# Limiting the record scatters of a mixture-of-experts kernel to two in flight

## The chip, the cores and the metric

The kernel runs on one core of one Trainium2 chip. The metric is the device time of one execution in microseconds (us). The kernel before took 806.48 us (median of 3 runs, 805.17 to 807.34). Five engines matter: PE (TensorE, matrix products), DVE (VectorE), ACT (ScalarE), POOL (GpSimd) and SP (SyncE, which here only issues DMA transfers). They run their own instruction streams and meet at semaphores.

## The reference, cut to what matters

The input has 4 x 1024 = 4096 rows of 256 values. A cross-attention block comes first, then a feed-forward block with 8 experts, of which each row uses two, and one shared expert that every row uses:

```
x = x + xattn(layernorm(x), ctx, ...)
xf = layernorm(x).reshape(-1, D)
scores = softmax(xf @ gate_w.T)
_, idx = top_k(scores + gate_b, 2)
rw[t, idx] = scores[t, idx]
h = silu((xf @ w1 + b1) * (xf @ w3 + b3))
oe = h @ w2 + b2
y = sum over e of rw[t, e] * oe[t, e]
z = expert(xf, sw1, sb1, sw3, sb3, sw2, sb2)
x = x + y + z
```

## The kernel before, in words

The rows are cut into NT = 32 tiles of 128. The attention stage works tile by tile and writes, for each tile, the result row block and its normalised copy (`xn2`) to DRAM. The router then works on all 32 tiles at once on DVE: softmax of the gate products, the two best experts of a row, and for each row and each of its TOP = 2 choices a **slot** in a table of 71 units of 128 places. A unit is a tile of 128 gathered rows that all go to one expert. There are NU = 2 * 32 + 7 = 71 units.

The **record scatter** (lines 621 to 629, POOL) writes the table. `record[:, t, k, :]` has, for each of 128 rows, eight bytes: the row's number and its weight. One indirect DMA puts the 128 records of one tile and one choice at their slots in the DRAM table `slots_scratch`; there are 32 * 2 = 64 such scatters, issued one behind the other. All of them add to one semaphore, `scat_out`. POOL then waits for all 64 and loads the table back with one DMA (line 629, semaphore `slots_in`).

The **feed-forward stage** is a software pipeline of steps over 103 tiles: 20 shared tiles first (R0 = 20), then the 71 routed units, then the last 12 shared tiles. In step s, PE does for tile s - 4 the second product (line 1092, three terms and three chunks, weights ws2 or w2), for tile s the transpose of its input (line 1239), for tile s - 3 the transpose of the hidden values (line 1247), and for tile s - 1 the first product (line 1092 again, 12 matmuls, weights ws13 or w13). ACT and DVE take each result from PSUM: ACT line 812 and DVE line 951 make the high and low part of the transposed input, DVE lines 969 and 972 add the bias and multiply, ACT line 822 is silu, ACT line 817 and DVE line 956 split the hidden values, and DVE line 945 adds a shared tile's result to its row block. PE signals each of its results with a semaphore (`Y_ok`, `X_ok`, `H_ok`, `UV_ok`).

Beside the first steps, SP loads the weights of the eight experts (lines 481 to 487, issued from 325.8 us on) and their biases (line 490), and ACT (lines 785, 787) and DVE (lines 992, 995) split those weights.

For routed units POOL gathers the rows (line 634), six units ahead: gather u waits on `X_ok` for tile 20 + u - 7, and the first gather also needs the loaded table, since it comes behind line 629 and its wait on POOL. Later POOL adds results to DRAM (line 641) between gathers. So the order on POOL is: 64 scatters, the table load, six gathers, then pairs of scatter-add and gather.

Of the kernel before, what the change touches and what calls it, by code (L numbers as in the profile page):

```python
# [20 lines left out]
def wait(eng, sem, n):  # L21

    if not isinstance(n, int) or n > 0:
        eng.wait_ge(sem, n)


def xattn_moe(nc, x, ctx, Wq, Wk, Wv, Wo, bo, gate_w, gate_b, w1, b1, w3, b3, w2, b2,
              sw1, sb1, sw3, sb3, sw2, sb2, out):
    B, N, D = x.shape
    _, NK, DC = ctx.shape  # L30
    INNER = Wq.shape[1]
    DH = 64
    HEADS = INNER // DH
    E, _, H = w1.shape
    TOP = 2
    T = B * N
    NT = T // P
# [33 lines left out]
    with stack:  # L71
        def sb(name, shape, dt, on=stack):
            return on.enter_context(nc.sbuf_tensor(name, shape, dt))

        def sem(name):
            return stack.enter_context(nc.semaphore(name))
# [7 lines left out]
        record = sb("record", [P, NT, TOP, 2], I32)  # L84
# [211 lines left out]
        rank_ok = sem("rank_ok")  # L296
        slot_ok = sem("slot_ok")
        eid_ok = sem("eid_ok")
        scat_out = sem("scat_out")
        slots_in = sem("slots_in")  # L300

        raw_in = [sem(f"raw_in{e}") for e in range(E)]
# [90 lines left out]
        def w_pieces(kind, j, name):  # L393

            if kind == "O":
                return [{"raw": wo_raw, "high": woh, "low": wol}[name][:, j, :]]
            w = {"K": {"raw": wk_raw, "high": wkh, "low": wkl}, "V": {"raw": wv_raw, "high": wvh, "low": wvl}}[kind][name]
            return [w[0:n, i, j * P:(j + 1) * P] for i, (_, n) in enumerate(KC)]
# [123 lines left out]
        def _(pool):  # L522
# [99 lines left out]
            pool.wait_ge(slot_ok, 1)  # L622
            for t in range(NT):
                for k in range(TOP):
                    pool.indirect_dma_start(slots_dram, bass.IndirectOffsetOnAxis(ap=slot[:, k, t:t + 1], axis=0),  # L625
                                            record[:, t, k, :], None).then_inc(scat_out, 16)

            pool.wait_ge(scat_out, 16 * TOP * NT)
            pool.dma_start(slots[:, :, :], slots_dram.rearrange("(p n) c -> p n c", p=P)).then_inc(slots_in, 16)

            def gather(u):
# [671 lines left out]
```

## Time and profile before

| what | value |
|---|---|
| median of 3 runs | 806.48 us |
| the profiled execution's own time | 811.39 us |
| its span, first to last instruction | 809.5 us |
| mean granted TensorE clock | 0.934 |
| PE busy | 675.1 us, 83% |
| DVE busy | 535.4 us, 66% |
| ACT busy | 396.9 us, 49% |
| POOL busy | 423.1 us, 52% |

The profile is of one execution. Its own time is what the device reports for that run, and 1.9 us of it lie outside the span. Times in the rows count from the start of the span. A row of the timeline has the start in us, the duration in us, the engine, the line, the operation, the destination and source, and in brackets the idle time of the engine before it with what ended the wait. "Issue" is time in which the engine waited for nothing that the profile shows; "remote" is a semaphore that arrived from a source or at a time that the profile can't tie to an instruction's end. DMA rows name the queue: q1 carries the transfers issued by SP, q0 those issued by POOL.

### The profile page before, as it was taken

How to read it: one execution, taken by the hardware profiler on the slowest of the kernel's cores; microseconds unless marked ns; L12 is line 12 of the kernel's file. 1: busy time of each engine (PE TensorE's matmuls, PEld its weight loads, DVE VectorE, ACT ScalarE, POOL GpSimd, SP SyncE). 2: the span in 40 equal slices, each digit the busy share in tenths (PEclk: the TensorE clock that was granted, in tenths of full speed). 3: DMA queues.
4: the chain of work that ended last, by engine and by line, in shares of the span. 5: the costliest groups of instructions: out<-in, count | busy, mean ns of one | idle time of the engine just before them, and what ended most of it. 6: DMA issues, size and time to landing. Idle time of an engine off the chain costs nothing.

```text
span 809.5 us, 16280 instructions
## 1 busy us (share of the span) xinstructions
PE 675.1 (83%) x4635; PEld 633.8 (78%) x4636; DVE 535.4 (66%) x1053; ACT 396.9 (49%) x1287; POOL 423.1 (52%) x532
## 2 busy tenths in 40 slices
PE   3996899999999996603007888999999999999995
PEld 2785799999999985602007878999999999999994
DVE  3884888888888874810008888666666666666678
ACT  3995777787778772301007322343444434434432
POOL 4353866556556643377750120667667777676300
PEclk9997999999999999765558999999999999999998
DMA  9202333222222212990002321344444444445595
GB/s 214 80 1 104 129 126 88 77 66 79 66 75 71 66 56 85 296 335 11 1 4 82 106 80 53 60 79 72 72 71 72 77 69 73 73 83 109 88 370 227
DMA packets 65005, 79.96 MB, mean 99 GB/s; under 512 B 11337, under 2 KB 57906, under 8 KB 64946
## 3 DMA queue, kind: packets, MB, share of 16 engines
q1 hardware_dynamic: 47618, 55.81, 22.7%
q0 software_dynamic: 15744, 18.84, 14.7%
q10 hardware_dynamic: 1584, 4.59, 1.5%
q8 instruction: 30, 0.49, 0.2%
q14 instruction: 29, 0.24, 0.1%
HBM read 49.97 MB, written 29.24 MB: 98 GB/s over the span
## 4 chain that ended last, share of the span: by engine, by line
PE 74%; another core or an unknown queue 9%; DVE 8%; issue 3%; DMA 3%; ACT 2%; POOL 1%; SPq 0%; ACTq 0%; DVEq 0%; POOLq 0%
PE ps L1092 62%; PE ps L1247 4%; PE ps L1175 3%; PE ps L1239 2%; PE ps L1152 1%; DMA wq_sb<-in_L_xattn_Wq 1%; DMA xrow<-xn_scratch,slots 1%; DVE w13l L992 1%; DVE uv L969 1%; PE ps L1194 1%; PE ps L1165 1%; DVE hTl L956 1%; DVE hmax L862 0%; DVE w2l L995 0%
## 5 line engine op out<-in xcount | busy, mean ns | idle before, releaser
L641 POOL DMA_INDIRECT acc_scratch<-yrow,slots x71 | 111.5, 1570 | 87.6 <-ACT yrow L802 84.0
L634 POOL DMA_INDIRECT xrow<-xn_scratch,slots x71 | 70.8, 997 | 74.3 <-PE ps L1239 54.5
L802 ACT ACTIVATE yrow<-ps,slots 128x256 f32<-128x256 f32 x71 | 33.7, 474 | 148.1 <-PE ps L1092 148.1
L812 ACT ACTIVATE uxTh<-ps 128x256 fp32r<-128x256 f32 x103 | 38.9, 378 | 133.7 <-remote 71.9
L1092 PE MATMUL ps<-w13h,uxTh 128*128 x284 | 97.5, 343 | 0.0
L1092 PE MATMUL ps<-ws2h,hTh 128*128 128x256 f32 x96 | 29.4, 306 | 78.9 <-DVE hTl L956 55.0
L969 DVE TENSOR_TENSOR uv<-ps,b 128x704 f32<-128x704 f32 x71 | 63.3, 891 | 47.5 <-PE ps L1092 46.8
L1092 PE MATMUL ps<-w13l,uxTh 128*128 x284 | 91.7, 323 | 0.0
L1092 PE MATMUL ps<-w13h,uxTl 128*128 x284 | 91.3, 321 | 0.0
L1092 PEld LDWEIGHTS ps<-ws2h,hTh 128*128 128x128 f32 x96 | 19.0, 197 | 83.7 <-DVE hTl L956 59.5
L625 POOL DMA_INDIRECT slots_scratch<-record,slot x64 | 62.0, 969 | 33.8 <-issue 19.2
L700 ACT ACTIVATE prob<-ps,nmax 128x64 f32<-128x64 f32 x256 | 76.3, 338 | 3.1 <-DVE nmax L865 3.1
L951 DVE TENSOR_TENSOR uxTl<-ps,uxTh 128x256 fp32r<-128x256 f32 x103 | 43.6, 423 | 48.0 <-ACT uxTh L812 43.9
L1092 PE MATMUL ps<-Uh,pTh 128*128 128x256 f32 x256 | 74.9, 293 | 0.0
L1092 PE MATMUL ps<-Uh,pTl 128*128 128x256 f32 x256 | 72.3, 282 | 0.0
L1092 PE MATMUL ps<-Ul,pTh 128*128 128x256 f32 x256 | 71.9, 281 | 0.0
L566 POOL TENSOR_TENSOR prob<-prob,hinv 128x1024 f32<-128x1024 f32 x32 | 61.0, 1905 | 13.0 <-DVE hinv L844 13.0
L1092 PE MATMUL ps<-Ah,xTh 128*128 128x512 f32 x128 | 57.2, 447 | 8.1 <-DVE xTl L875 8.1
L1092 PE MATMUL ps<-w2h,hTh 128*128 x213 | 63.0, 296 | 0.0
L956 DVE TENSOR_TENSOR hTl<-ps,hTh 128x384 fp32r<-128x384 f32 x103 | 57.3, 556 | 7.5 <-issue 7.4
L969 DVE TENSOR_TENSOR uv<-ps,bs 128x704 f32<-128x704 f32 x32 | 28.4, 889 | 50.8 <-remote 31.8
L1092 PE MATMUL ps<-w2l,hTh 128*128 x213 | 60.1, 282 | 0.0
(206 smaller groups left out, 2250.7 us busy)
## 6 DMA issues: line engine op xcount, KB each, us to landing
sums<-acc_scratch SPq DMA_DIRECT2D x16, 512.0 KB, 10.0
w_raw<-in_L_ffn_w SPq DMA_DIRECT2D x16, 352.0 KB
xin<-in_x SPq DMA_DIRECT2D x32, 128.0 KB, 2.5
acc_scratch<-yrow ACTq DMA_DIRECT2D x8, 512.0 KB, 2.7
xres<-in_x SPq DMA_DIRECT2D x32, 128.0 KB, 2.4
acc_scratch<-x SPq DMA_DIRECT2D x32, 128.0 KB, 1.9
xn_scratch<-xn SPq DMA_DIRECT2D x32, 128.0 KB, 2.4
xrow<-xn_scratch SPq DMA_DIRECT2D x32, 128.0 KB
```

What stands on the lines that cost most here:

```text
L566: pool.tensor_tensor(heads, heads, hinv[:, p, :].unsqueeze(2).to_broadcast([P, HEADS, NK]), ALU.mult).then_inc(norm_ok, 1)
L625: pool.indirect_dma_start(slots_dram, bass.IndirectOffsetOnAxis(ap=slot[:, k, t:t + 1], axis=0), record[:, t, k, :], None).then_inc(scat_o ...
L634: pool.indirect_dma_start(xrow[:, m, :], None, xn2_dram, bass.IndirectOffsetOnAxis(ap=slots[:, u, 0:1], axis=0)).then_inc(gather_in[m], 16)
L641: pool.indirect_dma_start(acc_dram[u % 2], bass.IndirectOffsetOnAxis(ap=slots[:, u, 0:1], axis=0), yrow[:, m % YRING, :], None, compute_op ...
L700: act.activation(prob[:, p, h * NK:(h + 1) * NK], ps[:, s_bank(p) + h // 8, h % 8 * NK:(h % 8 + 1) * NK], ACT.Exp, bias=nmax[:, p, h - HS: ...
L802: act.activation(yrow[:, y, :], ps[:, 6 + m % 2, 0:D], ACT.Copy, scale=slots[:, bass.ds(u, 1), 1].bitcast(F32)).then_inc(y_ok, 1)
L812: act.activation(uxTh[:, p, :], ps[:, 0, 0:D], ACT.Copy).then_inc(uxTh_ok, 1)
L951: dve.tensor_tensor(uxTl[:, p, :], ps[:, 0, 0:D], f32(uxTh[:, p, :]), ALU.subtract).then_inc(uxTl_ok, 1)
L956: dve.tensor_tensor(hTl[:, :], ps[:, 5, 0:H3], f32(hTh[:, :]), ALU.subtract).then_inc(hTl_ok, 1)
L969: dve.tensor_tensor(uv[:, :, :], ps[:, 1 + 2 * p:3 + 2 * p, 0:H], bias, ALU.add).then_inc(bias_ok, 1)
L1092: last = pe.matmul(out, stationary(k, a), moving(k, b), start=(k == 0 and i == 0), stop=(k == n - 1 and i == len(PARTS) - 1))
L1247: last = pe.transpose(ps[:, 5, k * P:(k + 1) * P], hid[:, p, k * P:(k + 1) * P], ident[:, :])
```

## The change

POOL waits, before each scatter, for the one two places back in the order: scatters of choice 0 and of choice 1 have a semaphore each, and scatter (t, k) waits until the t earlier ones of its own k have landed. The wait before the table load is then on both semaphores. Nothing else is altered. For t = 0 there is no wait, as the helper `wait` leaves out one for zero.

```diff
-        scat_out = sem("scat_out")
+        scat_out = [sem(f"scat_out{k}") for k in range(TOP)]
...
             for t in range(NT):
                 for k in range(TOP):
+                    wait(pool, scat_out[k], 16 * t)
                     pool.indirect_dma_start(slots_dram, bass.IndirectOffsetOnAxis(ap=slot[:, k, t:t + 1], axis=0),
-                                            record[:, t, k, :], None).then_inc(scat_out, 16)
-
-            pool.wait_ge(scat_out, 16 * TOP * NT)
+                                            record[:, t, k, :], None).then_inc(scat_out[k], 16)
+
+            for half in scat_out:
+                pool.wait_ge(half, 16 * NT)
             pool.dma_start(slots[:, :, :], slots_dram.rearrange("(p n) c -> p n c", p=P)).then_inc(slots_in, 16)
```

## Rows read from the trace of the kernel before

**Rows 1.** The page: the span in 40 slices of 20.24 us.
```profile
span 809.5 us, 16280 instructions
...
PE   3996899999999996603007888999999999999995
...
POOL 4353866556556643377750120667667777676300
PEclk9997999999999999765558999999999999999998
DMA  9202333222222212990002321344444444445595
```

**Rows 2.** Windows view: busy us (count) of PE, PEld, DVE, ACT, POOL; clock, DMA, GB/s.
```profile
342.00:346.00 4.00, 4.00 (x30) 3.74 (x28) 0.00 (x0) 1.67 (x3) 3.08 (x4) 1.00 1.09 326
346.00:366.00 20.00, 0.03 (x1) 0.00 (x0) 2.27 (x4) 0.38 (x1) 15.12 (x17) 0.61 1.00 316
366.00:418.00 52.00, 7.19 (x26) 6.00 (x26) 1.97 (x3) 2.96 (x5) 39.18 (x41) 0.53 0.03 2
418.00:427.00 9.00, 0.00 (x0) 0.00 (x0) 0.78 (x2) 0.77 (x3) 0.61 (x1) 0.50 0.10 26
427.00:457.00 30.00, 26.16 (x173) 25.59 (x174) 25.50 (x44) 18.68 (x36) 0.00 (x0) 0.91 0.30 87
```

**Rows 3.** Timeline of PE, 345 to 387 us.
```profile
345.70 0.32 PE L1092 MATMUL ps<-ws13l,uxTh 128*128 128x352 f32 x1
369.95 0.58 PE L1092 MATMUL ps<-ws2h,hTh 128*128 128x256 f32 x1 [23.92 <-issue]
...
371.82 0.41 PE L1092 MATMUL ps<-ws2l,hTh 128*128 128x256 f32 x1
372.04 0.63 PE L1239 MATMUL ps<-ident,xrow 128*128 128x128 f32 x2
...
374.69 0.32 PE L1092 MATMUL ps<-ws13h,uxTh 128*128 128x352 f32 x1
376.50 0.32 PE L1092 MATMUL ps<-ws13h,uxTl 128*128 128x352 f32 x1 [1.49 <-issue]
378.60 0.45 PE L1092 MATMUL ps<-ws13l,uxTh 128*128 128x352 f32 x1 [1.78 <-issue]
...
386.30 0.45 PE L1092 MATMUL ps<-ws13l,uxTh 128*128 128x352 f32 x1 [2.35 <-issue]
```

**Rows 4.** Timelines of ACT and DVE: the results of PE that arrived late.
```profile
361.09 0.38 ACT L812 ACTIVATE uxTh<-ps 128x256 fp32r<-128x256 f32 x1 [17.41 <-remote]
...
426.23 0.38 ACT L812 ACTIVATE uxTh<-ps 128x256 fp32r<-128x256 f32 x1 [54.45 <-remote]
...
401.71 0.89 DVE L969 TENSOR_TENSOR uv<-ps,bs 128x704 f32<-128x704 f32 x1 [31.82 <-remote]
...
424.81 0.42 DVE L945 TENSOR_TENSOR yrow<-ps,yrow 128x256 f32<-128x256 f32 x1 [21.65 <-remote]
```

**Rows 5.** Line 625: the group, then its first ones and what follows its last one.
```profile
L625 POOL DMA_INDIRECT slots_scratch<-record,slot x64: 963/967/1138, 336.1 to 416.4; - x64
...
336.12 1.14 POOL L625 DMA_INDIRECT slots_scratch<-record,slot  x1 [14.58 <-DVE slot L1063]
337.57 0.99 POOL L625 DMA_INDIRECT slots_scratch<-record,slot  x1 [0.31 <-issue]
338.86 0.97 POOL L625 DMA_INDIRECT slots_scratch<-record,slot  x1 [0.30 <-issue]
340.13 0.97 POOL L625 DMA_INDIRECT slots_scratch<-record,slot  x1 [0.30 <-issue]
...
416.41 0.97 POOL L625 DMA_INDIRECT slots_scratch<-record,slot  x1 [0.30 <-issue]
418.81 0.61 POOL L629 DMA_DIRECT2D slots<-slots_scratch  x1 [1.43 <-DMA slots_scratch<-record,slot]
```

**Rows 6.** DMA view, windows 336:341, 336:342, 336:348, 336:360, 336:366, 366:418, in this order.
```profile
q1 hardware_dynamic: 1441, 1.68, 107.7%
slots_scratch<-record,slot POOLq DMA_INDIRECT x4
...
q0 software_dynamic: 32, 0.00, 0.6%
slots_scratch<-record,slot POOLq DMA_INDIRECT x5
...
q0 software_dynamic: 191, 0.01, 1.3%
slots_scratch<-record,slot POOLq DMA_INDIRECT x10
...
q0 software_dynamic: 511, 0.02, 1.7%
...
slots_scratch<-record,slot POOLq DMA_INDIRECT x19
...
q0 software_dynamic: 708, 0.02, 1.8%
...
slots_scratch<-record,slot POOLq DMA_INDIRECT x24
...
q0 software_dynamic: 1320, 0.04, 2.1%
q1 hardware_dynamic: 71, 0.06, 0.5%
...
slots_scratch<-record,slot POOLq DMA_INDIRECT x41
```

**Rows 7.** Timelines: the first gather; PE's input transposes of tiles 19, 20.
```profile
457.19 1.08 POOL L634 DMA_INDIRECT xrow<-xn_scratch,slots  x1 [37.77 <-PE ps L1239]
...
462.08 0.96 POOL L634 DMA_INDIRECT xrow<-xn_scratch,slots  x1 [3.80 <-PE ps L1239]
...
488.30 0.38 PE L1239 MATMUL ps<-ident,xrow 128*128 128x128 f32 x2
491.85 0.38 PE L1239 MATMUL ps<-ident,xrow 128*128 128x128 f32 x2
```

**Rows 8.** Timeline of DVE, line 951: tiles 12 and 18 of the pipeline, six steps apart.
```profile
459.31 0.41 DVE L951 TENSOR_TENSOR uxTl<-ps,uxTh 128x256 fp32r<-128x256 f32 x1
...
486.19 0.41 DVE L951 TENSOR_TENSOR uxTl<-ps,uxTh 128x256 fp32r<-128x256 f32 x1
```

## The prediction

> **What bounds the kernel now.** I read the page's 40 slices first, then a table of windows around the hole they show, the timelines of PE, ACT and DVE in that hole, then POOL's timeline and the DMA view. PE is at 8 or 9 tenths in nearly every slice but those from about 324 to 425 us [rows 1]. From 342 to 346 us PE is busy all the time; from 346 to 366 us it does 0.03 us of work, from 366 to 418 us 7.19 us, and from 427 us on it is at 26.16 of 30 us again [rows 2]. So some 80 us hold little more than one step of the pipeline. POOL is the engine that works there: its 64 record scatters run from 336.12 to 417.4 us, and PE comes back soon behind them [rows 5, 2].
>
> The hole isn't missing data. PE's input transposes for tile 5 ran at 372.04 us, and ACT, which reads them, starts at 426.23 us, 54 us later; the first product that ended at 346.0 us is read by DVE at 401.71 us, the second product that ended at 372.2 us at 424.81 us [rows 3, 4]. PE's own instructions, which wait for nothing there, come 2.1 to 2.8 us apart [rows 3], where later 173 of them fit in 30 us, 0.17 us each [rows 2]. So while the scatters land, what PE signals arrives tens of us late and PE itself crawls. I call this the crawl. It begins between 342 and 346 us, a microsecond or so behind the first scatter's packets, and ends by 424.8 us, 6.0 us after the last scatter had landed. No row says why; that the scatters cause it is my reading of the two coincidences.
>
> **How many scatters are in flight now.** A scatter makes 32 packets on q0 (64 of them make 2048 in all, and 336:342 has exactly 32 where 336:341 has none). So the first one, issued at 336.12, moved between 341 and 342 us: its latency is 4.9 to 5.9 us, although nothing of its own queue was ahead of it; q1 is at over 100% then [rows 6]. By 348 us 10 were issued and 191 / 32 = 6.0 had moved: four in flight; by 360 us 19 against 16.0: three; by 366 us 24 against 22.1: two. From 366 to 418 us 41 were issued and 1320 / 32 = 41.3 moved, so it stays at two. The last one took 418.81 - 416.41 = 2.40 us from its start to POOL's next instruction, waking included [rows 5].
>
> **The change, part by part.** It adds 62 waits on POOL, takes none away, and adds one semaphore. The limit can only bind where the latency is above two issue intervals, 2 x 1.27 = 2.54 us [rows 5].
> - From about 364 us on, the latency is 2.40 us, so the wait is met when POOL gets to it: 0 us, with 0.14 us to spare. The bound from above: if a met wait still costs the 0.30 us that stands between two scatters [rows 5], once for each of some 25 pairs, that is 7.5 us. I take 0, since the 2.40 us has such a start in it.
> - Before that it binds. Two scatters per latency: with 5.5 us (the middle of 4.9 to 5.9) and 0.3 us to start the next, pairs go at 336.1, 341.9, 347.7 and 353.5 us, then with about 5.2, 4.2 and 3.0 us (the shrinking backlog of rows 6 times 1.27 us) at 358.7, 362.9 and 365.9 us. The scatter numbered 12, counted from 0, starts at 365.9 us; now it starts at 336.1 + 12 x 1.27 = 351.4 us. That is 14.5 us. Part of the latency is shorter when fewer records share the engines and the weights land a bit earlier, so I take 13 us (bounds 0, if the latency fell to 2.5 us, and 15).
> - Queued behind POOL's waits are only the other scatters, the table load and the gathers. The table lands near 434 us instead of 421 us. The first gather starts at 457.19 us for another reason, PE's transposes [rows 7], so the table has 36 us of cover, less what PE gains. If that cover is gone, the table decides (first rival).
> - PE, in the crawl until 6 us after the last scatter, is released 13 us later.
> - Against this: from 336 to 363 us 12 scatters are issued instead of 21, in bursts of two with gaps of some 3 us. If the crawl follows their density, PE gets work done in the gaps. A step of the pipeline takes (486.19 - 459.31) / 6 = 4.48 us here [rows 8]. Between no step and all five that fit in 346 to 368 us, I take one, -4.5 us: PE already stood after the first few scatters, so a pair is enough to bring it on.
>
> Sum: +13 - 4.5 = +8.5 us. The profiled execution took 811.39 us with a span of 809.5 us, so it would take some 819.9 us; the runs have a median of 806.48 us, 4.9 us below the profiled one, and I add the same to it: 815.0 us. Nothing behind 500 us changes, since the routed stage starts from the same point later.
>
> On the latency, the rows show 4.9 to 5.9 us under the weight load and 2.40 us without it [rows 5, 6]. The Trainium skill's page "DMA: Bandwidth & Descriptors", section "Anatomy of one DMA — SWDGE (gpsimd) path", gives a fixed cost of about 2.0 us that scales with nothing. By that rule a pair would always be back in time, the limit would never bind, and the sum would be 0: 806.5 us. The rows at 336 to 342 us speak against it for the part where it matters, and for it from 366 us on.
>
> **The rivals.**
> 1. *The crawl doesn't come.* It may need more than a couple of scatters piled up behind the weight load, and then hold itself as long as scatters flow. Price: PE would run its steps from 346 us at 4.48 us each and reach tile 20 at 346 + 15 x 4.48 = 413 us. There it waits for the table: landed at 434 us, the first gather and its landing bring the transposes of tile 20 to about 437.5 us, against 491.85 us now [rows 7]. 54 us less: 752 us. The point from which it decides is whether one scatter per 1.27 us is more than the shared path can take by itself. For it: the crawl began with four in flight and q1 full, and the step from promptness to standstill took two or three scatters. Against it: from 366 to 418 us only two were in flight and q1 was empty, and PE crawled all the same [rows 3, 6]. The change leaves that stretch as it is.
> 2. *The crawl comes late.* PE works at nearly its pace from 346 to about 368 us and stands after that. Four to five steps gained, 18 to 22 us, against 13 us lost: 797 to 802 us, or 799 us in the middle. For it: half the density in that stretch. Against it: the first few scatters were enough to delay a result by 17 us [rows 4].
> 3. *The limit doesn't bind* (it doesn't do what it says). The latency under the limit falls to 2.5 us because its own records were part of it. Then 806.5 us, no change. Against it: the first scatter had nothing ahead in its queue and took over 4.9 us.
> 4. *Waiting costs more.* No step gained, 15 us of shift and 7.5 us for the met waits: 829 us. It is the forecast's own upper end, and a small part of its chance.
>
> **How the numbers follow.** About 0.3%, 2.4 us, is what a measurement of this kernel can tell from no change. I give the forecast, with everything from +3 to +22 us, 0.44; rival 1 0.27; rival 2 0.17; rival 3, with sums that happen to cancel, 0.12. Faster is 0.27 + 0.17 = 0.44, same 0.12, slower 0.44. The likeliest case is 815 us; its own range is 809 to 824 us. To hold 8 in 10 the whole range must reach rival 1, so it goes from 750 to 824 us.
>
> **What would show it.** In the profile of the changed kernel line 625 should stand in pairs about 5.5 us apart until some 354 us, and then 1.27 us apart; the last one should start near 429 us and the table load near 432 us. Results of PE should again reach ACT and DVE tens of us late, with a hole in PE's slices that ends near 438 us. The first gather should still be released by PE's line 1239. Rival 1 is right if the hole is filled from 346 us and the first gather follows line 629 at once, rival 2 if four or more input transposes stand between 346 and 370 us, rival 3 if the last scatter starts before 418 us. The forecast is wrong in its main step if the scatters end later by 13 us and PE isn't held until then.

## The result, and the profile after

The changed kernel takes 774.74 us (median of 4 runs, 774.12 to 776.57). The kernel before took 805.87 us beside it (4 runs, 805.17 to 807.34). The ratio is 0.9614, with a 95% interval from 0.9595 to 0.9634: 31 us, or 3.9%, faster. The prediction was 815.0 us, so it had the wrong sign. Its range, 750 to 824 us, held the time.

The profiled execution took 774.89 us with a span of 773.1 us. First the page of the changed kernel: the 40 slices, here of 19.3 us, and the chain that ended last.

```profile
span 773.1 us, 16281 instructions
...
PE   4996899999999999486884049999999999999995
...
POOL 5343765656656554124666743677677677676300
PEclk9997999999999999699998559999999999999998
...
PE 75%; DMA 12%; DVE 4%; POOL 4%; issue 3%; ACT 1%; SPq 0%; ACTq 0%; POOLq 0%; DVEq 0%
PE ps L1094 62%; DMA slots_scratch<-record,slot 9%; POOL slots_scratch L626 4%; PE ps L1249 4%; PE ps L1177 3%; PE ps L1241 2%; PE ps L1154 2%; DMA wq_sb<-in_L_xattn_Wq 1%; DMA xrow<-xn_scratch,slots 1%; PE ps L1196 1%; PE ps L1167 1%; DVE hmax L864 0%; DVE sums L985 0%; PE ps L1113 0%; ACT prob L702 0%
```

The wide hole of [rows 1] is half filled. What is left is in the slices 22 to 24 (4, 0, 4; counted from 1), and the chain now names the record scatters (9% as DMA, 4% as line 626 on POOL). Then the windows view of the changed kernel, in the same stretches and columns as [rows 2].

```profile
342.00:346.00 4.00, 4.00 (x31) 4.00 (x30) 3.11 (x8) 3.77 (x8) 0.89 (x1) 1.00 1.10 319
346.00:366.00 20.00, 13.66 (x87) 13.17 (x86) 12.70 (x21) 11.91 (x23) 8.23 (x8) 0.91 0.96 305
366.00:418.00 52.00, 42.14 (x299) 40.20 (x297) 44.80 (x77) 16.05 (x37) 31.23 (x30) 1.00 0.31 90
418.00:427.00 9.00, 0.00 (x0) 0.00 (x0) 1.87 (x3) 0.00 (x0) 6.01 (x6) 0.62 0.13 30
427.00:457.00 30.00, 1.13 (x6) 1.14 (x7) 0.00 (x0) 0.38 (x1) 20.41 (x23) 0.50 0.06 12
```

PE works 13.66 us from 346 to 366 us (0.03 before) and 42.14 us from 366 to 418 us (7.19 before). Then it stands, and its granted clock falls from 1.00 to 0.50, which is from 2.4 to 1.2 GHz. The count on POOL is the second thing to see: 30 scatters in 366:418, one per 1.73 us, where [rows 2] has 41, one per 1.27 us. The next fence is the timeline of POOL in the changed kernel.

```profile
334.19 1.14 POOL L626 DMA_INDIRECT slots_scratch<-record,slot  x1 [14.62 <-DVE slot L1065]
335.64 0.99 POOL L626 DMA_INDIRECT slots_scratch<-record,slot  x1 [0.30 <-issue]
340.66 0.96 POOL L626 DMA_INDIRECT slots_scratch<-record,slot  x1 [4.04 <-DMA slots_scratch<-record,slot]
...
347.80 0.96 POOL L626 DMA_INDIRECT slots_scratch<-record,slot  x1 [4.91 <-DMA slots_scratch<-record,slot]
...
364.15 0.97 POOL L626 DMA_INDIRECT slots_scratch<-record,slot  x1 [1.51 <-DMA slots_scratch<-record,slot]
365.42 0.97 POOL L626 DMA_INDIRECT slots_scratch<-record,slot  x1 [0.30 <-issue]
367.59 0.97 POOL L626 DMA_INDIRECT slots_scratch<-record,slot  x1 [1.20 <-DMA slots_scratch<-record,slot]
369.73 0.97 POOL L626 DMA_INDIRECT slots_scratch<-record,slot  x1 [1.17 <-DMA slots_scratch<-record,slot]
...
447.76 0.96 POOL L626 DMA_INDIRECT slots_scratch<-record,slot  x1 [0.30 <-issue]
450.43 0.61 POOL L631 DMA_DIRECT2D slots<-slots_scratch  x1 [1.71 <-DMA slots_scratch<-record,slot]
452.83 1.01 POOL L636 DMA_INDIRECT xrow<-xn_scratch,slots  x1 [1.79 <-DMA slots<-slots_scratch]
```

The source view of line 626 of the changed kernel adds the waits up (idle us, times).

```profile
L626 POOL DMA_INDIRECT slots_scratch<-record,slot x64: 962/967/1679, 334.2 to 447.8; - x64
...
  DMA slots_scratch<-record,slot: 34.8, 19
```

The scatters go in pairs until 365 us, as predicted. After that the limit still binds, now and then, until 424 us; only from there, with PE standing, are the scatters 1.27 us apart. PE's timeline in the changed kernel shows who pays.

```profile
416.37 0.28 PE L1094 MATMUL ps<-ws2l,hTh 128*128 128x256 f32 x1
455.87 0.69 PE L1241 MATMUL ps<-ident,xrow 128*128 128x128 f32 x2 [39.22 <-DMA xrow<-xn_scratch,slots]
```

PE has done its shared tiles by 416.7 us, as the first rival said, and then waits 39.22 us for the first gather, which is behind the table, which is behind the last scatter. Tile 20 starts at 455.87 us instead of 491.85 us [rows 7]: 35.98 us earlier, and the span is 36.4 us shorter. So all but 0.4 us of the gain lies ahead of tile 20. (The median gained 31 us only, since the profiled execution of before, 811.39 us, was 5.5 us above its median and that of the changed kernel was not.)

### The profile page after: what moved, and what is told of

The parts are those of the page before. It is cut to its first block, busy times and chain, and to the rows that moved or that the text cites. A ratio compares the mean times of both kernels' runs of the same rounds, so it can differ in the third digit from the quotient of the medians.

```text
span 773.1 us, 16281 instructions
## 1 busy us (share of the span) xinstructions
PE 673.9 (87%) x4635; PEld 633.5 (82%) x4636; DVE 535.4 (69%) x1053; ACT 396.8 (51%) x1287; POOL 426.0 (55%) x532
## 3 DMA queue, kind: packets, MB, share of 16 engines
q0 software_dynamic: 15744, 18.84, 15.5%
## 4 chain that ended last, share of the span: by engine, by line
PE 75%; DMA 12%; DVE 4%; POOL 4%; issue 3%; ACT 1%; SPq 0%; ACTq 0%; POOLq 0%; DVEq 0%
PE ps L1094 62%; DMA slots_scratch<-record,slot 9%; POOL slots_scratch L626 4%; PE ps L1249 4%; PE ps L1177 3%; PE ps L1241 2%; PE ps L1154 2%; DMA wq_sb<-in_L_xattn_Wq 1%; DMA xrow<-xn_scratch,slots 1%; PE ps L1196 1%; PE ps L1167 1%; DVE hmax L864 0%; DVE sums L985 0%; PE ps L1113 0%; ACT prob L702 0%
## 5 line engine op out<-in xcount | busy, mean ns | idle before, releaser
L626 POOL DMA_INDIRECT slots_scratch<-record,slot x64 | 66.1, 1032 | 63.1 <-DMA slots_scratch<-record,slot 34.8
L1241 PE MATMUL ps<-ident,xrow 128*128 128x128 f32 x206 | 40.6, 279 | 49.3 <-DMA xrow<-xn_scratch,slots 39.4
L1241 PEld LDWEIGHTS ps<-ident,xrow 128*128 128x128 f32 x206 | 25.2, 142 | 50.6 <-DMA xrow<-xn_scratch,slots 39.4
L1094 PE MATMUL ps<-w2h,hTl 128*128 x213 | 60.0, 281 | 0.0
L702 ACT ACTIVATION_READ_ACCUMULATOR prob<-ps,nmax 128x1 f32 x256 | 59.4, 232 | 0.0
```

The source lines that it names most:

```text
L702: act.activation(prob[:, p, h * NK:(h + 1) * NK], ps[:, s_bank(p) + h // 8, h % 8 * NK:(h % 8 + 1) * NK], ACT.Exp, bias=nmax[:, p, h - HS: ...
L1094: last = pe.matmul(out, stationary(k, a), moving(k, b), start=(k == 0 and i == 0), stop=(k == n - 1 and i == len(PARTS) - 1))
L1241: last = pe.transpose(ps[:, 0, k * P:(k + 1) * P], xrow[:, m, k * P:(k + 1) * P], ident[:, :])
```

## The experiments

Eighteen runs were made, some of them of a kernel that had been run already. The times of before beside them were not always the same: it took 743 to 749 us on some occasions and 804.6 to 809.1 us on others. An occasion is here a moment at which before and some variants were run together, and each run is told with the time of before on its occasion. There are two exceptions: for the limit of three and for the small writes the record gives before's earlier runs on the same chip, 14 and 8 minutes older. Where no number of runs is given, it is one run.

**Split the semaphore, wait nowhere.** This is the change without its waits; n counts the scatters, TOP * t + k.

```diff
-        scat_out = sem("scat_out")
+        scat_out = [sem(f"scat_out{k}") for k in range(2)]
...
-                                            record[:, t, k, :], None).then_inc(scat_out, 16)
+                                        record[:, t, k, :], None).then_inc(scat_out[n % 2], 16)
```

> Edit: two semaphores as in the change, but no wait between scatters. Theory A (the wait's limit on the scatters in flight is what helps): this is the kernel before, 806 us within 3, scatters 1.27 us apart, PE idle from 346 to 425 us. Rival (one semaphore that counts to 1024 with 64 overlapping transfers is what delays the others): 775 us or less, the hole filled.

Measured: 746.42 us, beside a before of 743.26 us. The split itself costs 3 us at most, one run against one, but the pair is 60 us under the time that I had taken as before's. The last scatter starts at 418.6 us, PE makes the transposes of tile 20 at 427.3 us, and there is no crawl. So this run says nothing on the cause of the crawl. It says that the crawl isn't a fixed property of the kernel. (Its rival, that one semaphore counting to 1024 is what delays the others, is met by two later runs: the limit from 22 on has the two semaphores and crawls all the same, and the paced kernel has the single one and doesn't.)

**Limits of 4, 3 and 1.** The same code with 4, 3 or 1 semaphores and the wait ahead of each scatter (the changed kernel has it with 2).

```diff
+                wait(pool, scat_out[n % 4], 16 * (n // 4))
```

> Edit: four semaphores, scatter n waits for scatter n-4. Before 354 us some four were in flight without any limit, so this binds hardly at all. Theory A with a threshold (it is the pile of about four behind the weight load that starts the crawl): about as before, 800 us or more. Theory B (any backlog limit by landing lets PE's signals through, because POOL then yields when landings are late): between 755 and 785 us, the last scatter before 450 us.

> Edit: three semaphores, scatter n waits for scatter n-3. The question is first whether the kernel before crawls on this chip (806 us) or not (743 to 747 us). If it doesn't: every kernel so far ended 325 us behind its last scatter; with three in flight the limit binds only while the weights load (latency 5.5 us, so one scatter per 1.8 us for some 20 us, 8 us later in all) and seldom later: last scatter 428 to 432 us, 753 to 757 us. If it does: three in flight still fill PE's hole (below 785 us) if any limit does, or fall back to 800 us or more if only the limit of two is low enough.

> Edit: one semaphore, each scatter waits for the one before it. If the time after the change is set by the table (last scatter 447.8 us, first gather 452.8 us), then with one in flight the spacing is the latency: some 20 scatters at 5 us at most while the weights load, the rest at 2.4 to 3.5 us, so the last one starts near 334 + 6 x 5.5 + 57 x 2.9 = 530 us and the first gather some 5 us later: 850 to 860 us, slower than before. PE's signals prompt (under 4 us) throughout. Rival (the crawl comes from how many are in flight even at two, so one gives much more PE progress): can't beat this, since the table still comes late; it would show only in PE's delays.

Measured, all beside 743.26 us: 751.25 us (4 in flight), 758.66 us (3), 839.28 us (1). The last scatter starts at 423.8, 430.9 and 513.1 us. Where nothing crawls, each tightening only delays the table. Here is the source view of the scatters with one in flight.

```profile
  DMA slots_scratch<-record,slot: 116.6, 63
```

That is 1.85 us of waiting per scatter. This run also gives the latency of a lone scatter, since each starts when the one before has landed: the first three take 6.59, 6.84 and 6.52 us beside the weight load, those from 373 to 423 us, with PE and SP's row transfers at work for nearly all of that time, 2.38 to 3.58 us (mean 2.94 us), and from 425 us on, with PE standing and the DMA engines at 1% of their time, each takes 2.36 to 2.39 us. Three in flight came 1.7 us above what was expected, one 11 us below. Four came 3.8 us below the lower of its two ranges, both of which had been worked out for a before with a crawl.

**The limit on the first 16 scatters only, and on all but the first 22.** The second kernel has n >= 22 in place of n < 16.

```diff
+                if n < 16:
+                    wait(pool, scat_out[n % 2], 16 * (n // 2))
```

> Edit: the limit of two holds for the first 16 scatters only, the other 48 are free. Theory T (trigger: the crawl needs the pile-up behind the weight load and holds itself afterwards): no crawl, scatter 16 near 372 us, last one at 372 + 47 x 1.27 = 432 us, 758 to 762 us, faster than the change. Theory D (density: scatters at 1.27 us beside a working PE bring the crawl on by themselves): PE falls into the hole near 375 us and stays there to some 438 us, 790 to 805 us.

> Edit: the first 22 scatters are free as in the kernel before, the limit of two holds for the rest. Theory T: the pile-up happens, so where the kernel before crawls this crawls too, 800 us or more; theory D: PE works again from 364 us on, 775 us or less. Where nothing crawls: the last scatter between 416 and 435 us, 742 to 760 us.

Measured: 765.59 us beside 743.26 us, and 758.99 us beside 746.97 us. The two parts cost 22 and 12 us there (21 and 10 us when they were run again, below), together about what the limit on all of them costs (29 us, below). The first came 3.6 us above its range, the second within. Neither tells of the crawl, for the same reason.

**Both kernels again.** No edit.

> Edit: none, this is the kernel before, to get its trace beside the others. In the last four runs the kernel before took 743.3 us on its chip, not 806, and no variant showed the hole in PE's work. Theory P (the crawl belongs to the place or the moment of the run, not to the kernel): 743 us with the last scatter near 416 us and the first gather 5 us behind it, or 806 us with the hole, and the same for every unlimited variant of this call. Rival (the kernel before crawls always, and its single 743 us was an odd reading): 806 us.

> Edit: none, the kernel after. Where nothing crawls, all of e1 to e4 ended 325 us behind their last scatter. Theory P: 773 us (last scatter near 447 us, plus 325), with or without the crawl, so that the change costs 30 us where the kernel before takes 743 us, and gains 31 us where it takes 806 us. Rival: it gains everywhere, 745 us or less.

Measured: before 747.35 us (8 runs, 745.32 to 748.67) beside itself at 746.97 us (9 runs, 746.51 to 749.03), ratio 0.9996 [0.9981, 1.001]; the changed kernel 776.08 us (2 runs, 773.96 and 778.19) beside the same, ratio 1.0391 [1.0324, 1.0458]. Here are the windows view of before on this occasion (columns as in [rows 2]) and then its timelines of POOL and PE.

```profile
346.00:366.00 20.00, 13.96 (x88) 13.46 (x86) 12.93 (x22) 12.21 (x23) 15.43 (x16) 0.91 0.95 303
366.00:418.00 52.00, 41.89 (x297) 39.97 (x295) 44.80 (x76) 15.70 (x37) 40.41 (x39) 1.00 0.32 88
418.00:427.00 9.00, 0.00 (x0) 0.00 (x0) 1.56 (x3) 0.00 (x0) 3.79 (x4) 0.61 0.15 38
```

```profile
419.51 0.96 POOL L625 DMA_INDIRECT slots_scratch<-record,slot  x1 [0.30 <-issue]
423.38 0.61 POOL L629 DMA_DIRECT2D slots<-slots_scratch  x1 [2.91 <-DMA slots_scratch<-record,slot]
...
428.83 0.69 PE L1239 MATMUL ps<-ident,xrow 128*128 128x128 f32 x2 [12.49 <-DMA xrow<-xn_scratch,slots]
```

The same kernel, with the same scatters (39 in 366:418, one per 1.33 us), works through the stretch that was a hole in [rows 2]: 41.89 us of PE against 7.19 us. It reaches tile 20 at 428.83 us instead of 491.85 us. So the change has two effects of opposite sign. It takes 31 us off where before crawls, and it costs 29 us where before doesn't; its own time is 775 to 776 us on both occasions. The change makes the time independent of the occasion.

**No limit, but the scatters begin after the weights.** POOL waits for the experts' weights and biases, then issues freely. The theory here was that the crawl comes from scatters piled up behind the weight load, the stretch of [rows 6] with q1 at 107.7%.

```diff
+            for e in range(E):
+                pool.wait_ge(raw_in[e], 80)
+            pool.wait_ge(b13_in, 32 * E)
```

> Edit: no limit, but POOL waits for all the expert weights and biases to have landed (about 363 us) before the first scatter. It takes away the overlap of scatters with the weight load and nothing else. If the pile-up behind the weight load brings the crawl on (theory T): no crawl, last scatter near 363 + 63 x 1.27 = 443 us, 769 us. If 64 scatters at 1.27 us beside a working PE are enough (theory D): a hole from about 368 us on, 810 us or more. Where nothing crawls at all it can only say the 769 us.

Measured: 772.91 us beside 746.97 us, 3.9 us above what was expected. The first scatter starts at 361.42 us, the last at 445.9 us, and the time follows from that. No crawl, but before had none either: inconclusive for the crawl.

**Small writes from another engine.** Before, and SP writes a second set of the same 64 blocks of 8-byte records to DRAM, five beside each of its steps that load shared tiles, to see if it is the size of the writes that makes the crawl.

```diff
+                for _ in range(5):
+                    n = next(extras, None)
+                    if n is not None:
+                        sp.dma_start(extra_dram[n].rearrange("(p n) c -> p n c", p=P)[:, 0, :],
+                                     record[:, n // TOP, n % TOP, :]).then_inc(extra_out, 16)
```

> Edit: the kernel before, and beside it SP writes the same 64 blocks of 128 eight-byte records to a second DRAM table, five per pipeline step (plain DMAs, 0.43 us of SP each, 28 us in all), in the very stretch in which the scatters land. The output is the same. Theory W (eight-byte writes to DRAM, dense enough, are what keeps PE's signals back): the hole comes back also where the kernel before takes 743 to 747 us, and the time rises to 790 us or more. Rival (their density is not what does it): SP's row loads come a few us later, 743 to 757 us, PE's waits unchanged but for its loads.

Measured: 745.33 us beside 746.97 us. The writes start between 356 and 404 us, and PE is busy for 41.63 us from 366 to 418 us. On an occasion without a crawl these writes don't bring one. Whether they would on another wasn't tried.

**More shared tiles ahead, with and without the limit.** With 24 shared tiles first, PE has four more steps of cover for the table. This was to show whether the table bounds the changed kernel.

```diff
-    NA = 20
+    NA = 24
```

> Edit: the kernel before with 24 instead of 20 shared tiles ahead of the routed units (8 instead of 12 behind them). The work is the same. Where nothing crawls, e1 shows PE waiting 10 us for the first gather at tile 20; four more tiles, at 3.6 to 4.5 us each, cover that: 10 us less than the kernel before there, 734 to 739 us. Where it crawls: as the kernel before, 800 to 806 us, since the hole is not at tile 20.

> Edit: the kernel after with 24 instead of 20 shared tiles ahead. Its PE waits from about 418 to 456 us for the table; four more tiles at 3.6 to 4.5 us each move 14 to 18 us of work into that hole: 757 to 762 us, where the kernel after takes 774 to 776 us, with or without a crawl of the kernel before. If the table were not what bounds the kernel after, it would not move: 774 us.

This was an occasion on which before crawled (807.44 us, 7 runs). Free: 813.61 us (4 runs), ratio 1.0081 [1.0062, 1.01], 7.6 us above its range: it crawled too (PE 6.06 us from 366 to 418 us), and the four more tiles only added to it. With the limit of two: 769.63 us (4 runs), ratio 0.9525 [0.9501, 0.9549]. The second is a comparison at the same moment, with four runs each way, of the limit and its absence in otherwise equal kernels: 44 us. It missed its range of 757 to 762 us. The gain over the changed kernel's 774.74 us was 5 us instead of the 12 to 18 us expected, since with PE at work for longer the limit binds more often: 43.0 us in 24 waits instead of 34.8 us in 19. The last scatter starts at 452.5 us instead of 447.8 us, and the table still comes last (PE waits 26.43 us for the first gather).

**First 16 and from 22, twice more,** to meet an occasion on which before crawls.

> Edit: that of e4 once more (limit of two for the first 16 scatters only), looked for on a chip on which the kernel before crawls (806 us). There: theory T (the pile-up of scatters behind the weight load brings the crawl on and, once there, 1.27 us spacing keeps it): no hole, last scatter 438 us, 764 to 768 us. Theory D (scatters at 1.27 us beside a working PE are enough at any time): hole from about 380 us to 444 us, 790 us or more. If the kernel before takes 743 to 747 us here: 765 us again, and nothing is told apart.

> Edit: that of e8 once more (22 free scatters, then the limit of two). Where the kernel before crawls: theory T says that the crawl comes on and stays until the scatters end, since spacing in it is 1.27 us anyway (latency 2.40 us), 806 to 812 us. Theory D says the same for the time up to 364 us, and that the limit doesn't bind later, so the same again. Rival L (it is landing late that the wait answers to, so the limit lets PE out as soon as it holds): PE works from about 370 us on, 775 us or less. If the kernel before takes 743 to 747 us here: 759 us again.

> Edit and expectation as for e13: where the kernel before takes 806 us, theory T says 764 to 768 us and no hole, theory D a hole from about 380 to 444 us and 790 us or more. Where it takes 743 to 749 us: 765 to 770 us, nothing told apart.

> Edit and expectation as for e14: where the kernel before takes 806 us, theories T and D say 800 us or more, rival L 775 us or less. Where it takes 743 to 749 us: 759 us, nothing told apart.

The first time there was none: before 749.07 us, and 769.84 and 758.79 us for the two. The second time there was: before 807.55 us, first 16 limited 793.3 us, from 22 limited 806.19 us. Here is the run with the first 16 limited: its timelines of POOL, PE and ACT.

```profile
373.36 1.31 POOL L627 DMA_INDIRECT slots_scratch<-record,slot  x1 [3.00 <-DMA slots_scratch<-record,slot]
374.98 0.97 POOL L627 DMA_INDIRECT slots_scratch<-record,slot  x1 [0.30 <-issue]
376.25 0.97 POOL L627 DMA_INDIRECT slots_scratch<-record,slot  x1 [0.30 <-issue]
...
418.18 0.32 PE L1095 MATMUL ps<-ws13h,uxTl 128*128 128x352 f32 x1 [0.82 <-issue]
420.28 0.45 PE L1095 MATMUL ps<-ws13l,uxTh 128*128 128x352 f32 x1 [1.78 <-issue]
423.08 0.45 PE L1095 MATMUL ps<-ws13h,uxTh 128*128 128x352 f32 x1 [2.35 <-issue]
425.88 0.45 PE L1095 MATMUL ps<-ws13h,uxTl 128*128 128x352 f32 x1 [2.35 <-issue]
...
404.90 0.38 ACT L815 ACTIVATE uxTh<-ps 128x256 fp32r<-128x256 f32 x1 [16.15 <-remote]
```

The weight load is over by then (in the run that waits for it, it had ended by 361.42 us), the backlog never formed, and still the crawl comes, some 8 us after the scatters go free at 375 us: PE stands from 383.3 us. It has the marks of [rows 3] and [rows 4]: products 2.1 to 2.8 us apart, and ACT idle for 16.15 us until a result of PE. So a pile-up behind the weights isn't needed, and that theory falls. In the other run the crawl began, as in before, with the first scatters. Its windows view and the source view of its scatters are these.

```profile
342.00:346.00 4.00, 0.20 (x2) 0.00 (x0) 0.41 (x1) 0.00 (x0) 3.08 (x4) 1.00 1.09 334
346.00:366.00 20.00, 4.12 (x18) 4.12 (x19) 1.41 (x3) 3.35 (x6) 13.78 (x16) 0.51 0.79 247
366.00:418.00 52.00, 6.45 (x28) 5.91 (x27) 2.83 (x5) 3.35 (x6) 38.19 (x40) 0.53 0.05 9
```

```profile
L627 POOL DMA_INDIRECT slots_scratch<-record,slot x64: 962/967/1138, 332.3 to 414.6; - x64
...
  issue: 20.7, 62
...
  DMA slots_scratch<-record,slot: 0.6, 1
```

All 42 waits were there, and they cost little: 0.6 us by this view, and some 2 us by the starts, since the view puts the first of them, which let the backlog land (2.91 us from start to start), down to issue. With PE at a standstill a scatter lands in 2.40 us [rows 5], within the 2.54 us of two issues. So in this run the limit didn't end a crawl that had begun, as the prediction had argued for this stretch. What it does is to keep one from beginning. Beside a working pipeline the landings are later (2.38 to 3.58 us in the run with one in flight), and the limit then spaces the scatters.

**Space them without any wait for a landing.** If the rate is what matters, POOL can be slowed by work of its own: before, with one semaphore, and two fills of constants that nobody reads any more between the scatters. Beside it, four in flight once more.

```diff
+                    n = TOP * t + k
+                    if n:
+                        wait(pool, pace_ok, 2 * (n - 1))
+                        pool.memset(ones[:, :], 0.0).then_inc(pace_ok, 1)
+                        pool.memset(tri[:, :], 0.0).then_inc(pace_ok, 1)
```

> Edit: the kernel before, no limit, but two memsets of 128x128 on POOL (0.2 us each) between scatters, into tiles that nobody reads any more. The scatters come some 1.7 us apart instead of 1.27 us, from the first one on; their number in flight behind the weight load is 3 instead of 4. Theory D (in e15 the crawl came 10 us after scatters were freed to come 1.27 us apart; under the limit they came 1.7 us apart while PE worked, and no crawl came: it is their rate that decides): where the kernel before takes 806 us, no lasting hole, last scatter near 334 + 63 x 1.72 = 442 us, 766 to 775 us. Rival (it is POOL's answer to late landings that helps, not the rate): hole as before, until 6 us after the last scatter, 825 us or more. Where nothing crawls: 766 to 770 us.

> Edit: that of e2 once more (four in flight), looked for where the kernel before crawls. Theory D: with four allowed the scatters come 1.3 to 1.4 us apart even while PE works, so the crawl comes: 800 us or more. Rival (any limit does it): 751 to 760 us. Where nothing crawls: 751 us again.

Measured beside a before of 804.58 us: paced 760.8 us, four in flight 787.11 us. Both missed what was expected. The paced kernel came 5.2 us below its range, since its scatters were 1.59 us apart on average and not 1.72 us. Four in flight lies between the theory's 800 us and more and its rival's 751 to 760 us: the crawl came, but from 377 us on and not from 346 us. The chip was the one that had given 743.26 us for before on an earlier occasion. First the paced kernel: windows view, then timelines of POOL and PE.

```profile
346.00:366.00 20.00, 13.73 (x84) 12.77 (x82) 13.34 (x23) 12.63 (x23) 17.94 (x37) 0.91 0.94 302
366.00:418.00 52.00, 41.62 (x295) 39.98 (x295) 44.81 (x76) 15.35 (x36) 46.52 (x99) 1.00 0.31 86
```

```profile
334.97 1.00 POOL L631 DMA_INDIRECT slots_scratch<-record,slot  x1 [0.17 <-issue]
335.96 0.22 POOL L629 MEMSET ones<- 128x128 bf16 x1
336.11 0.22 POOL L630 MEMSET tri<- 128x128 bf16 x1
336.50 1.01 POOL L631 DMA_INDIRECT slots_scratch<-record,slot  x1 [0.17 <-issue]
...
433.62 0.98 POOL L631 DMA_INDIRECT slots_scratch<-record,slot  x1 [0.17 <-issue]
...
441.50 0.69 PE L1245 MATMUL ps<-ident,xrow 128*128 128x128 f32 x2 [25.74 <-DMA xrow<-xn_scratch,slots]
```

Then the windows view of the kernel with four in flight, and PE's timeline.

```profile
346.00:366.00 20.00, 13.30 (x90) 12.52 (x89) 14.14 (x23) 11.23 (x21) 12.79 (x12) 0.93 0.99 312
366.00:418.00 52.00, 21.84 (x111) 20.33 (x111) 12.07 (x21) 8.51 (x17) 39.42 (x41) 0.66 0.20 52
```

```profile
386.33 0.58 PE L1095 MATMUL ps<-ws2h,hTh 128*128 128x256 f32 x1 [9.03 <-issue]
```

The paced kernel has no limit and 33 scatters in 366:418 (99 instructions on POOL, a third of them scatters), one per 1.58 us. PE works through. With four in flight there are 41, one per 1.27 us, as in before; PE works until 377.3 us, then stands 9.03 us at once and comes back only in pieces (21.84 us of 52). Its scatters were one per 1.63 us from 342 to 366 us, where the limit bound, and PE worked; from 366 to 377 us they were one per 1.35 us, and the crawl followed. The number in flight doesn't sort these runs. Counted as the prediction counts it, from the packets on q0, here are the DMA view of the paced kernel from 325 to 360 us and that of the kernel with the first 16 limited from 325 to 380 us.

```profile
q0 software_dynamic: 448, 0.02, 1.0%
...
q0 software_dynamic: 574, 0.02, 0.8%
```

The paced kernel had started 17 scatters by 360 us and 448 / 32 = 14 had moved: three in flight behind the weight load, more than the limit of two lets pass, and PE worked. The other had started 19 by 380 us against 574 / 32 = 17.9: one in flight, just ahead of its crawl. So the runs speak for the spacing of the scatters as what keeps the crawl away, and for the number in flight only as far as it sets that spacing. On the occasions on which before crawls, this table holds all that was run (scatters counted in 366:418; the number beside it is 52 us divided by them or, for the two whose last scatter starts before 418 us, the mean distance of their starts):

| kernel | scatters in 366:418 | us apart | PE busy there | time |
|---|---|---|---|---|
| before | 41 | 1.27 | 7.19 us | 804.6 to 809.1 us |
| no limit, 24 shared tiles | 38 | 1.27 | 6.06 us | 813.6 us |
| limit from 22 on | 39 | 1.28 | 6.45 us | 806.2 us |
| limit on the first 16 | 38 | 1.37 | 25.77 us | 793.3 us |
| limit of four | 41 | 1.27 | 21.84 us | 787.1 us |
| paced | 33 | 1.58 | 41.62 us | 760.8 us |
| limit of two (the change) | 30 | 1.73 | 42.14 us | 774.7 us |
| limit of two, 24 shared tiles | 29 | 1.79 | 43.99 us | 769.6 us |

The kernels that crawled all had a stretch just ahead of it in which most scatters came freely, 1.27 us apart (from 375 us on in the one with the first 16 limited, a mean of 1.35 us in the one with a limit of four), so on such an occasion the spacing decides somewhere between 1.35 and 1.58 us. Where before doesn't crawl, 1.33 us is harmless. In the changed kernel the scatters were 1.27 us apart again from 424 to 448 us, but PE had nothing to do there, so a crawl couldn't have shown. The spacing rests on the paced kernel, which was run once; that one run escaped the crawl by chance isn't excluded, though none of the 13 runs of before and 4 of the free kernel with 24 shared tiles did on these occasions. The paced kernel is 14 us below the changed kernel's 774.74 us, measured at another moment, and 44 us below before; it is the best of those run where before crawls. Where before doesn't crawl it wasn't run. By the rule of the next section it would take about 761 us there too (an estimate from its last scatter, 433.6 us, and its 325.5 us), behind before's 747 us, so none of these kernels is best on both.

## Why the prediction was wrong

**What bounds the kernel without a crawl.** The time from the start of the last scatter to the end of the span is nearly a constant:

| kernel | last scatter starts | span | difference |
|---|---|---|---|
| split only | 418.6 | 744.6 | 326.0 |
| before, again | 419.5 | 746.9 | 327.4 |
| limit of four | 423.8 | 749.4 | 325.6 |
| limit of three | 430.9 | 756.9 | 326.0 |
| paced | 433.6 | 759.1 | 325.5 |
| after the weights | 445.9 | 771.1 | 325.2 |
| the change | 447.8 | 773.1 | 325.3 |
| limit of one | 513.1 | 837.5 | 324.4 |

Scatters, table, gather, tile 20: each is released by the one ahead. With the crawl before has 809.5 - 416.4 = 393.1 us, 68 us more. The others that crawled lie above it too: 354.6 us (first 16 limited), 361.6 us (limit of four) and 389.7 us (limit from 22 on).

Point by point:

- **The reading of now** was right for the profile that it was read from, and wrong in what it took for granted. The hole was taken for a fixed property of the kernel. It is one of two ways in which the same kernel runs, and one profile couldn't show that.
- **"It adds 62 waits; before 364 us it binds"** was right in kind. The scatter numbered 12 started 33.40 us behind the first (367.59 - 334.19), against 29.8 us predicted and 15.5 us in before. The latency was under-sized: three times in a row the pairs start 6.5, 7.1 and 6.7 us apart, not 5.8. The 4.9 to 5.9 us had ended with the moving of the packets. In the changed kernel the first scatter's packets had all moved by 339.8 us, 5.6 us after its start, and POOL, which waited for it, started the next at 340.66 us, 0.9 us later.
- **"From about 364 us on the wait is met: 0 us"** failed. The other 51 scatters took 447.76 - 367.59 = 80.17 us, against 51 x 1.27 = 64.8 us: 15.4 us more. The 2.40 us came from a row with PE at a standstill and 3% of the DMA engines' time in use [rows 2]. With the pipeline at work it is 2.38 to 3.58 us, as the run with one in flight shows. The run from 22 on shows that the argument was right under its own premise, some 2 us in 42 waits. In all the last scatter came 33.3 us later after the first one than in before, where 13 was predicted. I had taken a latency from a stretch whose condition the change itself would take away.
- **"PE, in the crawl until 6 us after the last scatter, is released 13 us later"** is the step that failed and that turned the sign. PE wasn't in a crawl at all: it worked 42.14 us from 366 to 418 us, where the forecast had the 7.19 us of before, and was done with its shared tiles 31 us ahead of the last scatter. What the prediction held against this, that the change leaves the stretch from 366 to 418 us as it is, fell with the point before: 30 scatters landed there, not 41.
- **"-4.5 us, one step gained"** was the smallest of what was there. Four steps ended between 346 and 369 us (ACT, line 814, takes a tile's transposes at 348.94, 354.36, 363.11 and 368.61 us), and the rest up to tile 19 followed.
- **The first rival** had the mechanism: the hole filled from 346 us, the shared tiles done at 416.7 us (413 us predicted), and the first gather straight behind the table. Its price was off by 22.7 us (774.7 against 752). 18.4 us of that is tile 20 at 455.87 instead of 437.5 us, since it took the forecast's 13 us for the scatters. Another 4.9 us is the correction from profiled run to median, which the changed kernel didn't need (774.89 us profiled, 774.74 us median), and from tile 20 on the changed kernel was 0.5 us quicker. Its point of decision, whether one scatter per 1.27 us is more than the shared path can take, is what the paced kernel speaks for, on an occasion with a crawl; on one without, before had 39 scatters in that stretch and no crawl. That a pile-up behind the weights is needed is refuted. That the crawl, once there, holds itself while scatters flow fits the run from 22 on.
- **The other rivals.** The second had PE stand again from about 368 us on, and it didn't. The third had a limit that doesn't bind, and POOL waited 34.8 us. The fourth kept the crawl and only added to its end.
- **The cover of the table**, 36 us, was named as what would decide if it went. It went, by 39.22 us of waiting.
- **"Nothing behind 500 us changes"** held: from tile 20 to the end it is 773.1 - 455.87 = 317.2 us, and was 809.5 - 491.85 = 317.7 us.

On the latency, the chip contradicted the page of the Trainium skill that the prediction weighed, "DMA: Bandwidth & Descriptors", section "Anatomy of one DMA — SWDGE (gpsimd) path", for this path. It has about 2.0 us fixed; by that rule the limit would never bind and the change would give 0. The changed kernel waited 34.8 us for landings, with pairs 6.5 to 7.1 us apart under the weight load. Only with PE and the weight queue idle was it near the rule, at 2.40 us in before and 2.37 us in the run with one in flight.

**What stays open.** No row shows what makes an occasion crawl, and whether before crawls can't be chosen. So the 31 us are the gain where it does, and not a gain of this kernel at all times. The crawl isn't a property of one chip, since the same one showed both, and within one comparison it stays (9 runs of before lay within 2.5 us of each other on one, 7 within 2.5 us on another). Nor does a row show which shared part the scatters and PE's signals meet in. In the run with the first 16 limited DVE's signals reach PE at once (DVE ends hTl at 388.96 and 412.27 us, PE starts at 389.01 and 412.33 us), so it is what comes from PE that is late; as the ends of matmuls are modelled, the rows can't tell a late signal from a matmul that really ended late. That the limit of two prevents the crawl is shown (four runs against four, twice). That it does so by the spacing rests on single runs. Why spacing should help is not shown.

## What to carry to other kernels

On some occasions an unlimited burst of small indirect scatters slows engines that have nothing to do with it, and putting some 0.3 us of other work between them may be worth more than a limit on how many are in flight, for less delay (one run here, 760.8 us against 774.74 us at another moment). When a profile shows a hole in which an engine's own instructions crawl with no wait, measure the kernel before at several moments ahead of explaining or removing it: here the same change was worth -31 or +29 us. And take a latency for a sum from a stretch in which the other engines do what they will do after the change.

## What the runs showed of the hardware that I had not expected

- The same kernel ran at 743.26 and at 804.58 us on the same chip at two moments. At the first, none of the variants beside it crawled; at the second, the one with a limit of four did.
- An indirect scatter of 128 8-byte records costs POOL 0.97 us to issue and 0.30 us to the next one. From start to a waiting POOL's next start it takes 6.5 to 7.1 us beside the full weight queue and 2.37 to 2.67 us with PE idle (450.43 - 447.76 in the changed kernel). The first isn't due to other scatters: with only one in flight it is still 6.52 to 6.84 us.
- When the crawl begins it isn't total: with four in flight PE still did 21.84 us of work in 52 us, in groups at normal pace with gaps of 9.03 and 18.86 us between them.
